# First convolution on 32x32 array tiles, from the quadratic maps where they lie

## Time and profile before

| | us |
|---|---|
| median of 3 runs | 373.39 (373.09 to 373.66) |
| span of the profiled execution, first to last instruction | 369.9 |
| first `padded` write (L729) ends | 8.18 |
| PE ends its last L0 matmul | 65.12 |
| second `padded` write (L729) ends | 72.60 |

### The profile page before, as it was taken

The page is one execution under the profiler, slowest core; times in us unless marked ns, Lnnn a source line. Parts: engine busy times, 40 slices in busy tenths (PEclk is TensorE's granted clock), DMA queues, the critical chain, the costliest instruction groups (busy, mean ns, idle before and its releaser), DMA issues.

```text
span 369.9 us, 5771 instructions
## 1 busy us (share of the span) xinstructions
PE 311.3 (84%) x2163; PEld 109.3 (30%) x2186; DVE 229.8 (62%) x494; ACT 173.0 (47%) x334; POOL 44.0 (12%) x44
## 2 busy tenths in 40 slices
PE   5599665688997556999999999999999799885994
PEld 1133111232342112333232323323232222333931
DVE  5980053834846662668786886777877221579945
ACT  2100000012335546978888787878878786300000
POOL 5000600400000000001010100101010102405100
PEclk9989966999999986999999999999999999998798
DMA  2799996000066953970000000000000000000001
GB/s 87 155 202 226 205 182 171 0 3 0 10 194 139 140 108 109 248 313 2 2 2 2 2 1 1 2 1 4 0 3 0 1 3 0 2 0 1 4 2 57
DMA packets 6283, 23.89 MB, mean 65 GB/s; under 512 B 1048, under 2 KB 1816, under 8 KB 5712
## 3 DMA queue, kind: packets, MB, share of 16 engines
q1 hardware_dynamic: 6000, 23.43, 26.3%
q0 software_dynamic: 256, 0.11, 0.2%
HBM read 11.59 MB, written 2.37 MB: 38 GB/s over the span
## 4 chain that ended last, share of the span: by engine, by line
PE 44%; DVE 10%; issue 5%; ACT 4%; another core or an unknown queue 0%; DVEq 0%; ACTq 0%
PE ps L1160 12%; PE ps L1178 12%; PE ps L1137 11%; DVE arena_a L461 3%; ACT arena_b L677 3%; PE ps L1290 2%; PE ps L1183 2%; PE ps L1233 2%; DVE mx L889 1%; PE ps L1250 1%; ACT relus L685 1%; DVE arena_a L965 1%; DVE sums L884 1%; PE ps L1298 1%; PE ps L1006 1%
## 5 line engine op out<-in xcount | busy, mean ns | idle before, releaser
L677 ACT ACTIVATE arena_b<-ps 128x512 f32<-128x512 f32 x232 | 125.2, 608 | 33.5 <-PE ps L1160 16.8
L1137 PE MATMUL ps<-arena_a 128*128 128x450 bf16 x256 | 86.1, 364 | 16.0 <-issue 11.5
L1160 PE MATMUL ps<-arena_a 128*128 128x512 bf16 x207 | 78.1, 386 | 1.0 <-ACT arena_b L677 0.4
L889 DVE TENSOR_REDUCE mx<-ps 128x1 f32<-128x450 f32 x120 | 69.2, 617 | 6.5 <-PE ps L1137 4.8
L884 DVE CUSTOM_DVE_ANT_0 sums<-ps,relus 128x450 bf16<-128x450 f32 x68 | 41.2, 625 | 40.5 <-PE ps L1137 31.1
L1178 PE MATMUL ps<-arena_b,vt 128*32 128x512 f32 x448 | 59.7, 605 | 0.7 <-ACT arena_b L677 0.7
L1160 PEld LDWEIGHTS ps<-arena_a 128*128 128x128 bf16 x224 | 21.6, 98 | 76.9 <-ACT arena_b L677 50.4
L685 ACT ACTIVATE relus<-ps 128x450 f32<-128x450 f32 x68 | 37.4, 556 | 11.0 <-PE ps L1137 10.9
L1006 PE MATMUL ps<-zeros 128*128 128x512 bf16 x109 | 29.0, 407 | 8.4 <-DMA xa<-x 3.5
L1137 PEld LDWEIGHTS ps<-arena_a 128*128 128x128 bf16 x256 | 23.8, 99 | 40.1 <-issue 10.7
L639 ACT ACTIVATE arena_b<-ps 96x386 f32<-96x386 f32 x3 | 1.5, 490 | 63.3 <-PE ps L1055 63.2
(11 more groups left out here) (131 smaller groups left out, 250.0 us busy)
## 6 DMA issues: line engine op xcount, KB each, us to landing
arena_b<-arena_a SPq DMA_DIRECT2D x12, 578.0 KB, 10.4
arena_b<-wmodes SPq DMA_DIRECT2D x1, 4096.0 KB, 22.0
arena_a<-k_scratch SPq DMA_DIRECT2D x3, 516.8 KB
arena_b<-arena_a SPq DMA_DIRECT2D x4, 306.0 KB, 5.6
arena_a<-q_scratch SPq DMA_DIRECT2D x3, 384.0 KB
arena_b<-arena_a SPq DMA_DIRECT2D x4, 272.0 KB, 5.0
k_scratch<-arena_b SPq DMA_DIRECT2D x3, 344.5 KB, 3.3
cst<-consts SPq DMA_DIRECT2D x1, 1029.0 KB, 11.1
```

Source lines behind the costliest of these rows:

```text
L677: nc.scalar.activation(probs[:, n % PRING, :], ps[:, SCORE_RING[n % len(SCORE_RING)], :], ACT.Exp).then_inc(expd, 1)
L889: nc.vector.tensor_reduce(mx[:, a, e:e + 1], bank, AX.X, ALU.max).then_inc(max_read, 1)
L1137: mm(ps[:, block_bank(i), 0:KHALF], qst[:, e, g, qt * P:(qt + 1) * P], kst[:, g, at:at + KHALF], start=True, stop=True).then_inc(max_score ...
L1160: last = mm(ps[:, bank, :], kst[:, g, t * P:(t + 1) * P], qst[:, e, g, :], start=True, stop=True)
```

## The change

What it does:

- The 16 maps become 13, without shifted copies and without a linear one: the linear taps read `xp`. The square is one ACT instruction, the 12 others are one DVE instruction of 1156 elements each.
- The copies into `arena_b` are gone, and with them all waits of SP, POOL and DVE on them. A tap is a matmul with 32 rows and 32 columns: image b on row group b, tap i on column group i mod 4. It writes bank 2b + e. So there are 54 x 4 x 2 = 432 matmul calls. e is now a half of the columns of the image. Taps 0 to 29 come in groups of four, both halves each; taps 30 to 53 first for e = 0, then for e = 1.
- The four column groups hold partial sums. ACT (b = 0, 2) and DVE (b = 1, 3) copy them from PSUM to `parts`, and PE adds them with a stacked identity (`osum`, 128 x 32), four matmul calls for each half, after all taps.
- DVE transposes, adds and takes statistics for each half. Its copies for the second half stand behind the whole work on the first half.
- DVE's memsets are gone. POOL does `xst` (4352), the ones (`k_words` = 11024 words) and the zeros (8192 words), one behind the other, after the second `l0_done`.
- The weights of L0 are an input of their own, tiled over four row groups, 54 x 32 words per partition, in two DMAs before the constants; the constants follow at once.

```diff
-            sp.dma_start(cst[:, 0:N_FIRST], consts[:, 0:N_FIRST]).then_inc(first_loaded, 16)
...
-            for t in range(1, len(TILES)):
-                sp.wait_ge(map_ready, SLOTS_PER_TILE * (t + 1))
-                if t == 3:
-                    sp.wait_ge(tile0_used, 1)
-                stack_tile(t, 0, NP, tile_in[t])
+            first = slice(0, FIRST_TAPS * 32)
+            rest = slice(FIRST_TAPS * 32, len(TAPS) * 32)
+            lw = l0w.rearrange("p s o -> p (s o)")
+            for i, cols in enumerate((first, rest)):
+                sp.dma_start(lw[:, cols], taps[:, cols]).then_inc(taps_loaded[i], 16)
+            sp.dma_start(cst[:], consts[:]).then_inc(consts_loaded, 16)
...
+            pool.wait_ge(l0_done, 2)
+            nc.gpsimd.memset(xst[:], 0.0).then_inc(xst_zeroed, 1)
+            pool.wait_ge(xst_zeroed, 1)
+            nc.gpsimd.memset(arena_a[64:P, q_words:q_words + k_words], TWO_ONES).then_inc(k_filled, 1)
             nc.gpsimd.memset(arena_a[64:P, 0:q_words], 0.0).then_inc(q_filled, 1)
...
+            nc.scalar.activation(maps[:, 0, :], xp[:, 0:NP], ACT.Square, scale=VOLTERRA_SCALE ** 0.5
+                                 ).then_inc(act_map, 1)
+            for e in range(2):
+                act.wait_ge(parts_done, e + 1)
+                for b in (0, 2):
+                    nc.scalar.activation(parts[:, e, b, :], ps[:, 2 * b + e, :], ACT.Copy).then_inc(parts_act, 1)
...
+            for e in range(2):
+                half = slice(e * HALF, (e + 1) * HALF)
+                dve.wait_ge(parts_done, e + 1)
+                for b in (1, 3):
+                    nc.vector.tensor_copy(parts[:, e, b, :], ps[:, 2 * b + e, :]).then_inc(parts_dve, 1)
+                dve.wait_ge(l0_done, e + 1)
+                nc.vector.transpose(l0t[:, half].rearrange("p (x o) -> p x o", o=32),
+                                    ps[:, e, :].rearrange("p (y x) -> p x y", y=32)).then_inc(l0_read, 1)
+                dve.wait_ge(l0_read, 2 * e + 1)
+                nc.vector.scalar_tensor_tensor(xb[:, half], l0t[:, half], c_("l0bias"), xa[:, half], ALU.add, ALU.add
+                                               ).then_inc(l0_read, 1)
+                dve.wait_ge(l0_read, 2 * e + 2)
+                link(nc.vector.bn_stats(stats[:, 6 * e:6 * e + 6], xb[:, half]))
+            dve.wait_ge(act_map, 1)
+            norm_from_stats(xb[:], interior(xp)).then_inc(padded, 1)
...
+            def l0_taps(taps_, e):
+                for i in taps_:
+                    m, py, px = TAPS[i]
+                    source = xp if m is None else maps[:, m, :]
+                    for b in range(B):
+                        r = slice(32 * b, 32 * b + 32)
+                        last = mm(ps[32 * (i % 4):32 * (i % 4) + 32, 2 * b + e, :].rearrange("p (y x) -> p y x", y=32),
+                                  l0w[r, i, :], window(source[r, :], py, px + 16 * e, 0, 32, 16), start=(i < 4),
+                                  stop=(i >= len(TAPS) - 4), skip_group_check=True)
...
+            for e in range(2):
+                pe.wait_ge(parts_act, 2 * e + 2)
+                pe.wait_ge(parts_dve, 2 * e + 2)
+                for b in range(B):
+                    last = mm(ps[32 * b:32 * b + 32, e, :], c_("osum"), parts[:, e, b, :], start=True, stop=True)
+                last.then_inc(l0_done, 1)
...
```

More of the change, by code:

```diff
@@ L52, with tap_list @@
 EPS = 1e-5
[L58 to L61, removed]
[4 rows of a table removed]
-]
-SLOTS_PER_TILE = P // C
-N_MAPS = SLOTS_PER_TILE * len(TILES)
-PLANE = 386
[L70 to L89, removed]
+OFFSETS = [(0, 0)] + [(0, dx) for dx in (1, 2)] + [(1, dx) for dx in (0, 1, -1, 2, -2)] + \
+    [(2, dx) for dx in (0, 1, -1, 2, -2)]
+N_KEPT = 45
+def tap_list():
+    taps = [(None, py, px) for py in range(3) for px in range(3)]
+    for m, (dy, dx) in enumerate(OFFSETS):
+        taps += [(m, py, px) for py in range(3 - dy) for px in range(3) if 0 <= px + dx <= 2]
+    return taps
+TAPS = tap_list()
+N_LINEAR = 9
+BOTH = 30
+assert len(TAPS) == N_LINEAR + N_KEPT
+FIRST_TAPS = 18
+PLANE = 386
 VOLTERRA_SCALE = float(np.float32(1.0 / np.sqrt(N_KEPT)))
@@ L229, with build @@
     N_CONST += _n
-def build(nc, x, consts, wmodes, out):
+def build(nc, x, taps, consts, wmodes, out):
     ctx = ExitStack()
@@ L327, in build @@
         map_ready = sem("map_ready")
-        tile0_top = sem("tile0_top")
-        tile_in = [sem(f"tile_in{t}") for t in range(len(TILES))]
+        parts_done = sem("parts_done")
+        parts_act = sem("parts_act")
+        parts_dve = sem("parts_dve")
         l0_done = sem("l0_done")
@@ L750, in _ @@
[L750 to L767, removed]
-            dve.wait_ge(consts_loaded, 16)
+            for m, (dy, dx) in enumerate(OFFSETS):
+                if m:
+                    at = dy * WP + dx
+                    nc.vector.scalar_tensor_tensor(maps[:, m, :], xp[:, 0:NP], VOLTERRA_SCALE, xp[:, at:at + NP],
+                                                   ALU.mult, ALU.mult).then_inc(map_ready, 1)
@@ L1038, in _ @@
[L1038 to L1042 removed]
+            pe.wait_ge(taps_loaded[0], 16)
+            pe.wait_ge(padded, 1)
+            def l0_taps(taps_, e):
[7 more added lines that the diff above has]
+                                  stop=(i >= len(TAPS) - 4), skip_group_check=True)
+                return last
@@ new lines, in l0_maps @@
+            def l0_maps(i):
+                m = TAPS[i][0]
+                if m == 0:
+                    pe.wait_ge(act_map, 1)
+                elif m is not None:
+                    pe.wait_ge(map_ready, m)
+            for i in range(0, BOTH, 4):
+                group = range(i, min(i + 4, BOTH))
+                if FIRST_TAPS in group:
+                    pe.wait_ge(taps_loaded[1], 16)
+                l0_maps(i)
+                l0_maps(group[-1])
+                for e in range(2):
+                    l0_taps(group, e)
@@ new lines, in _ @@
+            for e in range(2):
+                for i in range(BOTH, len(TAPS)):
+                    if e == 0:
+                        l0_maps(i)
+                    last = l0_taps((i,), e)
+                last.then_inc(parts_done, 1)
+            pe.wait_ge(consts_loaded, 16)
+            for e in range(2):
+                pe.wait_ge(parts_act, 2 * e + 2)
[3 more added lines that the diff above has]
+                last.then_inc(l0_done, 1)
@@ L1379, in layout_consts, with layout_taps @@
     return c
+def layout_taps(i):
+    w1 = np.asarray(i["L0_conv_W1"]).reshape(C, 9, 32)
+    w2 = np.asarray(i["L0_conv_W2"]).reshape(C, 9, 9, 32)
+    out = np.zeros((C, len(TAPS), 32), np.float32)
+    for s, (m, py, px) in enumerate(TAPS):
+        dy, dx = OFFSETS[m or 0]
+        p, q = py * 3 + px, (py + dy) * 3 + px + dx
+        out[:, s] = w1[:, p] if m is None else w2[:, p, q]
+    return np.ascontiguousarray(np.tile(out.reshape(C, len(TAPS) * 32), (B, 1)))
 def kernel(**inputs):
```

102 lines of the change are left out of this document (16 added, 86 removed), and 4 rows, old and new, of the table TILES.

## The result

The changed kernel took 360.85 us, the median of four runs (359.95 to 361.68); the kernel before took 373.24 us on the same chip (372.94 to 373.66). The ratio is 0.9676, 95% interval 0.9651 to 0.9701: 12.4 us faster, where 17.2 were forecast. A repeat in a later comparison gave 358.11 us (356.18 to 359.32), ratio 0.960 [0.9552, 0.9648]. So the size of the gain is 12 to 14 us; reasons for single microseconds are taken from the traces, since the same kernel's median moved by 2.7 us between two sets of runs. What lies around a span is 2.2 us (359.95 against 357.8), and 1.8 to 2.3 us in the other runs, not the 3.5 us that were taken from before's median and span.

The account below looks back on a forecast made before the run. L0 was taken as bound by its map copies. The second `padded` moves from 72.6 to 53.7 us: 18.9 gained, 1.7 lost to a cold L1, 17.2 net, so 373.4 becomes 356.2 us; range 344 to 370.

Parts of the forecast that it names:

- The copies of the maps go, and PE's wait with them: Start of L0: PE's 3.97 us wait before L1024 goes; taps start at 8.7 us and never stall for a map.
- The taps, 24.1 us: L0's tap matmuls: four row groups overlap fully, so 28 rounds of 0.86 us take 24.1 us.
- the rival with three sizes: L0's taps: row groups overlap only partly; 48.2 or 92.9 us (chance 0.16, half rate or below), or 26 to 38 (0.08).
- the mild form: L0's taps: mild partial overlap, 26 to 38 us, giving 358 to 370 us in all; chance 0.08.
- the stated range: Whole kernel: 344 to 370 us, from no wait with a warm second sum up to mild partial overlap.
- the half rate: L0's taps: only neighbours overlap, a round needs four times 0.43 us; 48.2 us, 380.3 in all; half or below, chance 0.16.
- DVE's order: Between L0's two sums: DVE copies the second half late, PE idles 3.7 us, the second sum runs cold, 1.9 us.
- T: End of L0's second sum (e = 1), forecast at 39.6 us.
- The fill holds the normalisation: Second normalisation: DVE's store waits for POOL's running fill of ones, to T + 13.25; `padded` at 53.7 us; chance 0.50.
- Both rivals on it: Second normalisation: DVE does not wait (345.5 us, chance 0.17), or waits for both long fills (363.1 us, chance 0.09).
- The cold L1: Start of L1: after PE idles 9 us it begins at half clock, losing 1.7 us.
- The rest hidden: Behind the second `padded`: POOL's remaining fills, the constants and DVE's dropped memsets (9.3 us) stay covered.

Follow-up runs that it names:

- the kernel with both halves in a row: Against the version with the fills placed: calls e = 0 and e = 1 of one tap and image follow each other on one tile; 365.05 us.
- the copies first: Against the changed kernel: DVE's two copies of the second half's parts stand before its work on the first half; 355.23 us.
- The eight pieces: Against the changed kernel: POOL's memset of the ones (11024 words) is cut into 8 of 1378 words; 351.81 us, ratio to before 0.944.
- the further zeros: Against the changed kernel: 14 more zero matmuls on PE between the two sums and 38 more before L1; 354.67 us, ratio 0.9508.
- the version with the fills placed: Against the changed kernel: DVE's second-half copies first, POOL's fills placed around the normalisation stores, zeros in two halves; 343.63 us, ratio to before 0.9215.

## Why the prediction was right and wrong

**The copies of the maps go, and PE's wait with them: right.** L1024 is gone with its 3.97 us of idle and its cold start; the taps run from 9.05 (predicted 8.7; `x` came 0.35 us later) to 38.2 without a stall for a map.

**The taps, 24.1 us: the step that was mis-sized.** They took 29.1 us, 28 rounds of 1.04 instead of 0.86. This is 5.0 of the 5.1 us by which the gain in the spans was missed (17.2 forecast, 12.1 measured); the rest nearly cancels: `x` 0.35 late, the fill 0.35 sooner, 0.3 more for the cold clock. The medians missed by 4.8 us. The sentence that failed is "in L1024 four calls overlap although each has its second half waiting behind its first, so tiles queue by themselves": right for four tiles, and taken over to sixteen, with an issue rate of 29 ns a pair read from matmuls of one column. The rows could show that tiles queue, not how many pairs can stand in the queue. The runs show some 32 pairs, whose places come free only 0.19 us after the tile could have taken the next, and 12.8 of 16 tiles at work. Of the rival with three sizes, only the mild form came, at its lower part (26 to 38 us); it had a chance of 0.08, too little for what was an extrapolation. The time lies in the stated range because the range took in this case as well, not because the taps came as forecast. Row groups of one column group do overlap, so the half rate (48.2 us) did not come; the kernel with both halves in a row came to it by another mechanism. The Trainium skill (TensorE: Matmul & The Clock Gate, "Measured speedup vs the span model") has 10.6 for 16 tiles, from which 36.4 us were estimated (from one tile's 864 x 0.43 us the estimate would be 35.0). This trace gives 864 x 0.43 / 29.1 = 12.8. The measured number decides; the direction of the Trainium skill's figure was right.

**DVE's order: right.** From the end of the taps to T 6.65 us were predicted and 6.6 measured; the idle before the second sum was 3.77 against 3.7, the sum 1.81 against 1.9. With the copies first T came 3.9 us sooner.

**The fill holds the normalisation: right, in mechanism and size.** `padded` came at T + 13.75 (predicted T + 14.1). The Trainium skill's rule (SBUF — State Buffer, "Who interferes with whom"), that the one that comes second blocks, held where the rows of before had only the other direction: 9.41 us against 0.81. Both rivals on it fell: the wait exists, and DVE gets its turn between two fills. The eight pieces show that the length of the single instruction is what counts.

**The cold L1: right.** Predicted 1.7 us; from the second to the third `padded` it is 15.0 us against 12.99 before, 2.0. With the further zeros it is 12.6.

**The rest hidden: right.** From the third `padded` to the end it is 284.3 us in both profiles (369.9 - 85.6 and 357.8 - 73.5). That they agree to a tenth is luck: in the profiles of the ten runs it is 280.6 to 284.5 us.

The sum by the two traces: `padded` 72.6 - 58.5 = 14.1 gained, 2.0 lost, 12.1, which is the difference of the spans. In the version with the fills placed, the second `padded` is at 46.68 and the third at 59.27, 26.3 us earlier than before; its span is 27.6 less. The remaining 1.3 us lie behind the third `padded`, within that spread.

What stays open is the steady state of the queue, which was not followed pair by pair, and why the part behind the third `padded` differs by up to 4 us from profile to profile. That neighbours on one row or column group or the supply of instructions set the 1.04 us of a round is excluded.

## What to carry to other kernels

Packing small tiles pays only as far as the pairs in flight reach (here some 32): put different tiles next to each other in program order, never several pairs for one, and don't take the rate of four tiles for that of sixteen. A long fill on GpSimd is not free because GpSimd is idle: look which DVE stores from SBUF to SBUF fall into it, cut it into pieces, or put it beside DVE work that runs at its usual time with it (here copies from PSUM, transposes, additions and statistics). When a chain gets shorter, engines that it used to keep apart meet; here the third normalisation and the next fill did as soon as the second was free.

## What the hardware showed that was not expected

- Instructions arrive in transfers of 16 KB, one for 128 pairs of load and matmul, and with short matmuls PE pauses about 0.5 us at each: 27 ns a pair is the least that a long unrolled stretch reached, against 33.7 in the full kernel.
- Load and matmul pairs on 32x32 tiles in fp32: 12.8 tiles of 16 at work with two in a row on each tile, 7.6 with four in a row, 56 ns a pair instead of 33.7; 11.6 of 12 where only 12 tiles take turns.
- 32 loads go out at once where the first 32 pairs lie on 16 tiles, 17 where they lie on eight. Matmuls on different tiles do not start in the order of the program: eight tiles' first matmuls started within 0.1 us, ahead of the second to fourth of the first tile.
- After the same 3.77 us of idle a sum of eight matmuls ran mostly at half clock (1.81 to 1.94 us), once in between (1.50) and once at full clock (1.07).
- DVE's tensor_scalar of 1024 fp32 elements took 9.41 us behind a GpSimd memset, 1.38 behind one of an eighth of its length, 0.81 alone. Between two memsets that follow without a wait DVE gets its turn, and the second memset shows the time as its own (7.47 instead of 6.93 us).
